# Cross-attention: the first two pairs of key tiles multiplied by the values in one visit

## The reference, cut to what matters

```
kv = layernorm(src) @ ed_wkv;  k2, v2 = heads(split(kv))        # 750 keys
q2 = heads(layernorm(result) @ ed_wq)                           # 224 queries
wei2 = softmax(q2 @ k2.T * scale)                               # per head 224 x 750
result = result + merge(wei2 @ v2) @ ed_wproj + ed_bproj
```

## Time and profile before

| | |
|---|---|
| median of 3 runs | 1501.54 us (1499.16 to 1502.66) |
| the profiled execution | 1497.26 us, of which its span is 1495.4 us |
| PE busy over the span | 1352.8 us (90%), weight loads 1113.9 us (74%) |
| DVE, ACT, POOL busy | 826.8, 667.8, 654.1 us (55, 45, 44%) |
| granted TensorE clock, mean | 0.955 of full speed |
| cross-attention, 864 to 1430 us | PE busy 544.85 of 566 us, clock 1.00 |
| cross-attention, 1430 to 1495 us | PE busy 48.14 of 65 us, clock 0.75 |

### The profile page before, as it was taken

How to read it: one execution, slowest core, us unless ns; L and a number is a source line. 1 busy time by engine, 2 the same in 40 slices (tenths; PEclk the granted TensorE clock), 3 DMA queues, 4 the chain that set the end, 5 groups by cost and what they waited for, 6 DMA issues and landing times.

```text
span 1495.4 us, 26115 instructions
## 1 busy us (share of the span) xinstructions
PE 1352.8 (90%) x9689; PEld 1113.9 (74%) x9689; DVE 826.8 (55%) x2056; ACT 667.8 (45%) x1622; POOL 654.1 (44%) x547
## 2 busy tenths in 40 slices
PE   6899999995999999998458899999989999999986
PEld 5699988984878888887347676777867677777853
DVE  4421222242477677788325767676675767666551
ACT  4322211241556666565023555463645546374431
POOL 3133322340444555553420455554554445555563
PEclk9999999997999999998768999999999999999996
DMA  5301110034636555654346765566647656665520
GB/s 172 131 22 43 42 42 21 28 129 132 120 68 146 147 131 125 150 122 141 95 80 83 122 89 106 84 103 117 86 91 106 111 85 107 103 94 72 93 36 26
DMA packets 97056, 142.13 MB, mean 95 GB/s; under 512 B 9521, under 2 KB 62553, under 8 KB 95945
## 3 DMA queue, kind: packets, MB, share of 16 engines
q1 hardware_dynamic: 96944, 140.67, 46.8%
HBM read 59.40 MB, written 22.02 MB: 54 GB/s over the span
## 4 chain that ended last, share of the span: by engine, by line
PE 35%; DMA 6%; DVE 4%; ACT 3%; POOL 1%; issue 1%; POOLq 0%; SPq 0%; ACTq 0%
PE ca_ps_acc L1411 16%; PE ca_ps_p L1428 5%; DMA ctx_tokens<-in_ctx_dram 5%; PE ca_ps_s L1441 5%; PE ca_ps_o L1455 5%; PE ca_ps_acc L1504 3%; DVE ca_xT L1394 2%; DVE ca_maxes L1360 1%; ACT ca_f L1329 1%; DMA ca_k_stack<-ca_keys 1%; ACT ca_xT L1323 1%; PE ca_ps_o L1470 1%; POOL ca_partial L1275 1%; ACT ca_probT L1296 1%; PE ca_ps_acc L1496 0%
## 5 line engine op out<-in xcount | busy, mean ns | idle before, releaser
L1275 POOL TENSOR_TENSOR ca_partial<-ca_partial,ca_probT 125x896 f32<-125x896 f32 x128 | 272.5, 2129 | 235.2 <-ACT ca_probT L1296 230.2
L1296 ACT ACTIVATE ca_probT<-ca_ps_p 125x448 f32<-125x448 f32 x384 | 209.8, 551 | 229.7 <-PE ca_ps_p L1428 228.4
L1360 DVE TENSOR_REDUCE ca_maxes<-ca_ps_s 112x1 f32<-112x375 f32 x512 | 253.2, 540 | 84.4 <-PE ca_ps_s L1441 83.8
L1441 PE MATMUL ca_ps_s<-ca_k_stack,ca_q_stack 96*112 96x376 f32 x512 | 173.5, 368 | 34.8 <-DVE ca_maxes L1360 20.8
L1428 PEld LDWEIGHTS ca_ps_p<-ca_q_stack,ca_k_stack 98*125 98x125 f32 x768 | 132.9, 191 | 53.3 <-issue 41.0
L402 PE MATMUL ff_ps_y<-ff_w,ff_hT 128*128 128x512 f32 x672 | 161.0, 396 | 6.7 <-DVE ff_w L63 6.7
L1428 PE MATMUL ca_ps_p<-ca_q_stack,ca_k_stack 98*125 98x224 f32 x768 | 163.4, 297 | 3.2 <-ACT ca_probT L1296 3.0
L1411 PE MATMUL ca_ps_acc<-ca_xT,w_a 128*128 128x376 f32 x768 | 158.9, 345 | 6.7 <-DVE ca_xT L1394 6.7
L262 POOL TENSOR_TENSOR ff_hT<-ff_hrelu,ff_hT 128x256 fp32r<-128x256 f32 x112 | 86.1, 771 | 162.3 <-DVE ff_hT L345 162.3
L1411 PE MATMUL ca_ps_acc<-w_b,ca_xT 128*125 128x512 f32 x576 | 152.5, 401 | 0.8 <-DVE ca_keys L1389 0.8
L402 PEld LDWEIGHTS ff_ps_y<-ff_w,ff_hT 128*128 128x128 f32 x672 | 126.3, 191 | 33.3 <-issue 4.2
(11 more groups left out here) (131 smaller groups left out, 2388.4 us busy)
## 6 DMA issues: line engine op xcount, KB each, us to landing
ca_k_stack<-ca_keys SPq DMA_DIRECT2D x96, 376.0 KB, 8.0
ctx_tokens<-in_ctx_dram SPq DMA_DIRECT2D x8, 1500.0 KB
sa_Q_stack<-sa_rows SPq DMA_DIRECT2D x96, 112.0 KB, 3.4
sa_K_stack<-sa_rows SPq DMA_DIRECT2D x96, 112.0 KB, 3.7
ca_q_stack<-q_out SPq DMA_DIRECT2D x96, 112.0 KB, 10.0
ctx_tokens<-in_L_xattn_ff_w_dram SPq DMA_DIRECT2D x16, 512.0 KB, 4.5
q_out<-sa_yT SPq DMA_DIRECT2D x16, 448.0 KB, 3.6
ff_xin<-in_x_dram SPq DMA_DIRECT2D x7, 512.0 KB, 3.8
```

Of the source, the lines that this page charges most:

```text
L1275: pool.tensor_tensor(total, total, half(a), ALU.add).then_inc(partial_done, 1)
L1296: act.activation(probT[0:JT, step % PAIRS, u % GH].rearrange("p a t -> p (a t)"), ps_p[u % 2][0:JT, 0:2 * T], ACT.Exp).then_inc(exp_done, 1)
L1360: dve.tensor_reduce(maxes[:, q, j, a:a + 1], ps_s[n % 3][0:TQ, 0:JH], AX_X, ALU.max).then_inc(s_read, 1)
L1441: pe.matmul(ps_s[n % 3][0:TQ, 0:JP], q_stack[0:KS, h, TQ * q:TQ * (q + 1)], k_stack[0:KS, h, a, :], start=True, stop=True).then_inc(s_psum, 1)
```

## The change

In the plan the value of pair 0 no longer stands at the end of slot 7. At the end of slot 10 now stand both values, pair 0 and then pair 1. Nothing else in the list changes place, and the instructions of each value are the same.

```diff
-            if i in (7, 10) and 0 <= s - 3 < NG:
-                items.append(("value", s - 3, (i - 7) // 3))
+            if i == 10 and 0 <= s - 3 < NG:
+                items += [("value", s - 3, pair) for pair in range(2)]
```

## The result

The changed kernel takes 1523.63 us, the median of 6 runs (1513.33 to 1530.76); the kernel before took 1501.28 us in 6 runs beside it (1499.16 to 1503.78). The ratio is 1.0151, its 95% interval 1.0121 to 1.0181: **slower by 22 us**, where 4.9 us less was forecast. The profiled execution is one of 1519.18 us, its span 1517.4 against 1495.4, the mean granted clock 0.944 against 0.955.

What follows compares the result with a forecast made beforehand. The prediction took the order and density of PE's own stream as the bound. Terms -4.6 + 0 - 0.7 + 1.5 + 0.2 - 0.6 - 0.7 gave -4.9 us, 1501.54 to 1496.6 us, range 1491.0 to 1503.5.

Steps and rivals of the forecast that it cites:

- The seams: Entering and leaving a value visit on PE costs 0.13 + 0.20; one visit fewer saves 0.33 us, -4.6 over 14 steps.
- the wait that I argued away in rows 5: g = 2 step, score 8a: 6b is read by 1060.3, 8a would start at 1060.48, so no wait.
- So what PE does between T 11 and score 7b is free there.: Five g = 0 steps: the context's DMA, 16.38 us, then statistics set the path, and score 7b waits 0.57 us.
- SyncE issues nothing for a value; only the context's DMA waits for T 11: Waits that move: SyncE's only effect is the context's DMA behind T 11, already counted in the +1.5.
- After the other two K waits for VectorE's last differences, so 0.: Two of the seven g = 3 steps with T: a later T 11 costs nothing, 0.
- g = 3, T 11 0.3 later: g = 3 steps: T 11 ends about 0.3 later; five release the pacing DMA, +1.5 us (bounds 0 and +3.8).
- Rival C: The clock falls in g = 3 steps, merged visit 3.1 instead of 1.65 us: +5, 1506.6 us; chance 0.08.
- the miss by a hair: Five g = 0 steps behind the DMA: 8b just misses 7a's maximum, ends 0.33 late, cancelling the gain: 0.
- A: VectorE's maxima take the seams in g = 1 and 2 too: -1 to +1, 1501.5 us; chance 0.23.
- B: The g = 3 and g = 0 steps lose nothing: -8.1, 1493.4 us; chance 0.14.
- D: PE's weight queue hides the exit, only 0.13 saved a visit: about -0.7, 1500.8 us; chance 0.05.
- Step 31 and the end: Step 31, scores at VectorE's pace, +0.2; step 32 -0.6 if the clock is granted; steps 33 and 34 -0.7 together.

Runs made afterwards that it cites:

- m0: Values merged in the g = 0 steps alone, against the kernel before: 1499.92 us, ratio 1.0.
- m3: Values merged in the g = 3 steps alone, against the kernel before: 1522.1 us, ratio 1.0155.
- the hold: SyncE issues g = 0's `k_stack` DMA only once the next context has landed: changed kernel 1494.28 us; kernel before, batches 2 to 6 only, 1495.17 us.
- m12: Values merged in the g = 1 and 2 steps alone, against the kernel before: 1497.05 us, ratio 0.9976.
- the two split runs: Changed kernel with the context loaded in two halves, run twice: 1476.93 us, then 1474.99 us; ratios 0.9840 and 0.9838 to the kernel before.

## Why the prediction was wrong, by its own steps

- **The seams were right, a little too large.** Prob 8 and the visit stand in the chain as forecast (0.21 for prob 8, 1.65 for 32 instructions, 0.41 for the prob behind). A g = 1 step gained 0.29 and a g = 2 step 0.24, where 0.33 was costed: 14 steps -3.6 for -4.6. In the g = 2 step score 8a stands at 0.29 where 0.17 is usual: the wait that I argued away in rows 5 is there, at some 0.1 us. The chain of the changed kernel in a g = 2 step, from prob 8 on:

```profile
1067.58 0.21 PE ca_ps_p L1428 x2
1067.79 0.29 PE ca_ps_s L1441
...
1072.17 1.65 PE ca_ps_o L1455 x32
1073.82 0.41 PE ca_ps_p L1428 x2
```

- **The step that failed: "So what PE does between T 11 and score 7b is free there."** PE's time there is free, but when its work there is done is not: a K lies in that stretch, and this K feeds a DMA of 1.1 MB in the same queue as the load that paces the step. The sum had the load as a constant that merely starts 0.3 later: +1.5 in the g = 3 term and 0 (-1.7 to +0.5) in the term of the five g = 0 steps behind it, where +23.5 was measured. I wrote that "SyncE issues nothing for a value; only the context's DMA waits for T 11": true of what waits directly, and silent about the `k_stack` DMA, which moved by 0.8 us relative to the load, and the load grew by 1.6 to 3.3 us. The row had warned: the waits of score 7b ran from 0.57 to 2.2 us in one profile, so the load's length varied already, and I did not ask with what. Nor did I look at the clock behind the wait of 2.2 us, which was at 0.66 over 5 us in the kernel before; I had reckoned with a fall in the g = 3 steps only.
- **"After the other two K waits for VectorE's last differences, so 0."** I took T_rest at its usual length. K's waits for it fell from 4.7 to 1.2 us, as one T_rest dropped from 1.59 to 0.53. By the traces this gain is what started the loss; no run changed T_rest alone.
- **g = 3, T 11 0.3 later.** At full clock the interval from the D to the context's issue grew by 0.35 (14.85 to 15.20), as forecast. The whole interval became 0.45 shorter (23.02 to 22.56), which I had put between 0 and +0.76: K's earlier start is in it.
- **Rival C was right in kind, and wrong in weight.** In three of the six g = 3 steps the clock fell, +1.4 to +1.6 us each, +4.7 of the 22. Against its working, the wait before score 10a did not grow (1.01 before, 1.00 after). The larger part of the low clock came from elsewhere: the stalls of 3.6 to 5.3 us at score 7b.
- **g = 0, the miss by a hair** (0, -1.7 to +0.5 for the five): m0, with the load undisturbed, has nothing measurable in the total, and from score 7b to the next D the step takes 12.25 us instead of 12.18, so what this term had of PE's own work held.
- **Rivals A, B and D.** A: no more waits than before, but for the 0.1 us in g = 2. B: it needed g = 3 and g = 0 to lose nothing. D: the prob behind a visit still takes 0.41 and prob 8 0.21, so the exit is a seam. The rule of the Trainium skill named in the prediction, read as hiding the exit, is not borne out here.
- **Step 31 and the end**, -1.1 forecast, +1.2 found. The same intervals sum to between 62.1 and 65.3 us over the profiles, with unmerged and merged visits alike; whether the merge costs or gains there is not settled.

**Why 0.8 us costs more than 0.8 us.** From its issue to the first statistics the load takes 14.6 to 15.3 us with the `k_stack` DMA held, 14.7 to 17.5 with it at +12.8 to +13.1 us, and 16.6 to 18.5 with it at +12.0 to +12.3. The traces also record each DMA packet, and the packets show what the load meets. The load is 125 packets of 12288 bytes, each 0.46 us when alone, and the first packet of `k_stack` (3008 bytes) starts 1.3 us after that DMA's issue. In the kernel before, at most one packet of the load is unfinished at that moment, and the last one ends 14.0 to 14.6 us after the issue. In the changed kernel and in m3, 6 to 11 are unfinished; the longest of them takes 1.3 to 2.0 us, and the last ends at 15.0 to 16.6. The statistics, too, begin later after that last packet: 0.5 to 0.9 us with the hold, 0.7 to 1.8 before, 1.5 to 2.2 in the changed kernel and m3. So those 0.8 us took the `k_stack` DMA from just behind the load's tail into it. In the m12 profile the `k_stack` DMA stands at +13.1 (+12.8 once) as before; up to two packets were unfinished, and three loads took 17.5, 16.1 and 15.9 us. Why a packet that meets the others takes three to four times as long, and why the signal of its end comes later, stays **open**.

The packets show one thing more that I had overlooked: the load never has more than 7 packets in flight, the `k_stack` DMA up to 22, and the load's end is told by five signals. So fewer transfers run side by side in the DMA that paces the step than in the one that it meets. Whether another layout of its 125 rows would shorten it was not tried.

## What to carry to other kernels

When a transfer paces a step, its length is part of the prediction: list what else is issued while it is in flight and ask whether the change moves that nearer, even by less than a microsecond. Time gained off the critical path is not free, since it starts the next transfer sooner. And where a change that is sound by itself comes out slower, look at the collision before undoing it: here the merge was worth 6 us once the load was split, and splitting the load was worth 17 more.

## What I had not expected of the hardware

- The load of 1.5 MB took 14.6 to 15.3 us with the next DMA held, and up to 18.5 us when a DMA of 1.1 MB was issued 12.0 to 12.3 us in, whose first packet found 6 to 11 of the load's 125 packets unfinished.
- The same difference of 128x375 on VectorE took 0.53 to 0.55 us in most places, and 1.43 to 1.78 us where it began 0.9 us or more into one of GpSimd's additions.
- The same wait of 1.0 us before score 10a was followed by a lower granted clock in 7 of the 30 g = 3 steps with a merged visit (changed kernel 3, with hold 2, the two split runs 1 each, m3 none), and in none of the 42 with two visits (seven profiles).
- In the eight profiles with an unsplit load, score 7b waited 0.5 to 1.9 us in 27 of the 40 steps behind it, and the clock stayed at 1.00 up to the next D; in the other 13 it waited 2.1 to 5.3 us, and each time the clock there was lower, 0.78 to 0.88 in the mean.
